# One-expert network: first layer two and second layer four steps behind the transpose, with an unread product of the identity ahead of each

## The reference

```python
scores = jnp.einsum('bsh,he->bse', x, wr) + br
expert_id = jnp.argmax(scores, axis=-1)
h = jnp.einsum('bsh,ehf->ebsf', x, w1) + b1[:, None, None, :]
h = jax.nn.gelu(h, approximate=False)
y = jnp.einsum('ebsf,efh->ebsh', h, w2) + b2[:, None, None, :]
one_hot = jax.nn.one_hot(expert_id, E, dtype=x.dtype)
out = jnp.einsum('ebsh,bse->bsh', y, one_hot)
...
x = x + _L1_ffn_ref(_layernorm(x, axis=-1), L1_ffn_wr, L1_ffn_br, L1_ffn_w1, L1_ffn_b1, L1_ffn_w2, L1_ffn_b2)
```

## Time and profile before

| | us |
|---|---|
| median of 3 runs (1870.96 to 1874.24) | 1872.3 |
| the profiled execution, its own time | 1877.03 |
| its span, first to last instruction | 1875.2 |
| share of the span in which PE, DVE, POOL, ACT are busy | 86%, 76%, 75%, 51% |

### The profile page before, as it was taken

How to read it: one execution, slowest core, us unless ns; L and a number is a source line. 1 busy time by engine, 2 the same in 40 slices (tenths; PEclk the granted TensorE clock), 3 DMA queues, 4 the chain that set the end, 5 groups by cost and what they waited for, 6 DMA issues and landing times. The chain is left out here.

```text
span 1875.2 us, 63422 instructions
## 1 busy us (share of the span) xinstructions
PE 1620.9 (86%) x24719; PEld 1365.9 (73%) x24719; DVE 1422.6 (76%) x3215; ACT 952.6 (51%) x2012; POOL 1408.6 (75%) x1270
## 2 busy tenths in 40 slices
PE   4999999999989364999999999999997688277776
PEld 3888888777778253778888888888886588277676
DVE  6988888888876914889898888888885756755554
ACT  3777887777763323454454544444443610344443
POOL 3887787988975554899999998888885267766654
PEclk9999999999999576999999999999999789588888
DMA  8000050000000414444444343433342364522211
GB/s 256 12 10 9 9 190 14 20 17 17 18 8 1 135 38 123 114 115 116 122 108 108 96 97 97 97 97 97 97 98 49 92 216 145 171 65 62 61 57 35
DMA packets 155077, 154.08 MB, mean 82 GB/s; under 512 B 37246, under 2 KB 106944, under 8 KB 154160
## 3 DMA queue, kind: packets, MB, share of 16 engines
q1 hardware_dynamic: 128912, 125.14, 24.7%
q0 software_dynamic: 6704, 15.61, 2.9%
q10 hardware_dynamic: 19312, 11.48, 2.3%
HBM read 58.77 MB, written 26.71 MB: 46 GB/s over the span
## 5 line engine op out<-in xcount | busy, mean ns | idle before, releaser
L1455 POOL TENSOR_TENSOR wa_rot<-wa_rot,wa_cross 128x1024 f32<-128x1024 f32 x128 | 306.9, 2397 | 44.1 <-DVE wa_cross L1673 43.0
L417 POOL TENSOR_TENSOR sa_sd<-sa_sd,sa_mx 128x1024 f32<-128x1024 f32 x128 | 245.2, 1916 | 78.2 <-DVE sa_mx L665 77.8
L1670 DVE TENSOR_TENSOR wa_rot<-wa_ps_qk,cos 128x1024 f32<-128x1024 f32 x128 | 155.6, 1216 | 36.8 <-PE wa_ps_qk L1521 36.7
L1620 ACT COPY wa_pt<-wa_ps_svt 128x1024 f32<-128x1024 f32 x64 | 64.9, 1015 | 220.7 <-PE wa_ps_svt L1557 220.7
L665 DVE TENSOR_REDUCE sa_mx<-sa_sd 128x16 f32<-128x1024 f32 x128 | 154.8, 1209 | 0.0
L1461 POOL TENSOR_TENSOR wa_sd<-wa_sd,wa_mx 128x1024 f32<-128x1024 f32 x64 | 121.8, 1904 | 34.2 <-DVE wa_mx L1686 33.8
L545 PEld LDWEIGHTS sa_ps_o<-sa_vbd,sa_pt 128*64 128x64 f32 x4096 | 135.0, 138 | 11.5 <-issue 8.1
L1521 PE MATMUL wa_ps_qk<-wa_xt,l_wk 128*128 128x128 f32 x1024 | 134.5, 286 | 9.7 <-DVE wa_cross L1673 9.5
L545 PE MATMUL sa_ps_o<-sa_vbd,sa_pt 128*64 128x18 f32 x4096 | 139.2, 210 | 1.8 <-DVE sa_o L694 1.8
L1521 PE MATMUL wa_ps_qk<-wa_xt,l_wq 128*128 128x128 f32 x1024 | 134.2, 285 | 6.4 <-DVE wa_cross L1673 4.1
L534 PE MATMUL sa_ps_st<-ident,sa_sd 128*128 128x128 f32 x1024 | 135.8, 276 | 3.7 <-ACT sa_sd L606 1.5
(11 more groups left out here) (313 smaller groups left out, 4307.0 us busy)
## 6 DMA issues: line engine op xcount, KB each, us to landing
wa_whole<-wa_rot SPq DMA_DIRECT2D x1024, 64.0 KB, 2.0
choice_dram<-sa_zero_rows SPq DMA_DIRECT2D x32, 256.0 KB, 3.2
choice<-choice_dram ACTq DMA_DIRECT2D x22, 256.0 KB, 4.0
x_res<-in_x_dram SPq DMA_DIRECT2D x16, 256.0 KB, 6.7
sa_ctx_t<-in_ctx_t_dram SPq DMA_DIRECT2D x64, 64.0 KB, 1.8
c_index<-in_index_dram SPq DMA_DIRECT2D x2, 2048.0 KB, 7.7
xn_dram<-c_xn SPq DMA_DIRECT2D x16, 256.0 KB, 3.0
cs_ctx_t<-in_ctx_t_dram SPq DMA_DIRECT2D x16, 256.0 KB, 2.9
```

The lines of the kernel that those rows point to most:

```text
L417: pool.tensor_tensor(sd[:, v % 4], sd[:, v % 4], mx[:, v % 4].unsqueeze(2).to_broadcast([P, H0, SEQ]), ALU.subtract).then_inc(sub_ready, 1)
L1455: pool.tensor_tensor(rot[n][:, v % 2], rot[n][:, v % 2], cross[n][:], ALU.add)\
L1670: dve.tensor_tensor(rot[n][:, v % 2].rearrange("p f j t -> p (f j) t"), src.rearrange("p f j t -> p (f j) t"), bc(k.cos[:], 1, 2 * QUADS), ...
```

## The change

The first layer moves from one to two steps behind the transpose, the second from two to four. The transposed tile, the hidden layer and `ps_h` get four buffers instead of two (`ps_x`, `ps_y` and the weights keep theirs), and the waits for free buffers move with them. In front of each layer, between the wait for a free buffer and the wait for the data, stands a product of the identity with itself, which goes to the place in PSUM that the layer then overwrites; nobody reads it. DVE's final add moves from three to four steps behind, to stay with the second layer.

```diff
-        xt = sb("xt", [P, 2, P])
-        hid = sb("hid", [P, 2, FF, P])
+        xt = sb("xt", [P, 4, P])
+        hid = sb("hid", [P, 4, FF, P])
-        ps_h = [c.enter_context(nc.psum_tensor(f"m1_h{n}", [P, FF, P], F32)) for n in range(2)]
+        ps_h = [c.enter_context(nc.psum_tensor(f"m1_h{n}", [P, FF, P], F32)) for n in range(4)]
...
+            def keep_on(room):
+                pe.matmul(room, k.ident[:], k.ident[:], start=True, stop=True)
...
             def hidden(t, v):
+                if late(t, 4):
+                    pe.wait_ge(hid_ready, t - 3)
+                keep_on(ps_h[v % 4][:, 0])
                 pe.wait_ge(xt_ready, t + 1)
                 pe.wait_ge(wt_ready, t + 1)
-                if late(t, 2):
-                    pe.wait_ge(hid_ready, t - 1)
                 for f in range(FF):
-                    mm = pe.matmul(ps_h[v % 2][:, f], w1[:, v % 4, f * P:(f + 1) * P], xt[:, v % 2], start=True, stop=True)
+                    mm = pe.matmul(ps_h[v % 4][:, f], w1[:, v % 4, f * P:(f + 1) * P], xt[:, v % 4], start=True, stop=True)
...
             def output(t, v):
-                pe.wait_ge(hid_ready, t + 1)
                 if late(t, 2):
                     pe.wait_ge(y_ready, t - 1)
+                keep_on(ps_y[v % 2][:, 0:P])
+                pe.wait_ge(hid_ready, t + 1)
                 for f in range(FF):
...
-                for stage, behind in ((transpose, 0), (hidden, 1), (output, 2)):
+                for stage, behind in ((transpose, 0), (hidden, 2), (output, 4)):
...
-            pipeline(pe, NS, step, 2, DEEP)
+            pipeline(pe, NS, step, 4, DEEP)
...
             def x_copy(t, v):
                 act.wait_ge(xt_made, t + 1)
-                if late(t, 2):
-                    act.wait_ge(h_made, t - 1)
+                if late(t, 4):
+                    act.wait_ge(h_made, t - 3)
...
             def gelu(t, v):
                 act.wait_ge(h_made, t + 1)
-                if late(t, 2):
-                    act.wait_ge(y_made, t - 1)
+                if late(t, 4):
+                    act.wait_ge(y_made, t - 3)
...
-                for stage, behind in ((x_copy, 0), (gelu, 1)):
+                for stage, behind in ((x_copy, 0), (gelu, 2)):
...
-            for i in range(NS + 3):
+            for i in range(NS + 4):
...
-                if i >= 3:
-                    add_up(i - 3)
+                if i >= 4:
+                    add_up(i - 4)
```

More of the change, by code:

```diff
@@ L2289, in hidden @@
             def hidden(t, v):
+                if late(t, 4):
+                    pe.wait_ge(hid_ready, t - 3)
+                keep_on(ps_h[v % 4][:, 0])
                 pe.wait_ge(xt_ready, t + 1)
                 pe.wait_ge(wt_ready, t + 1)
-                if late(t, 2):
-                    pe.wait_ge(hid_ready, t - 1)
                 for f in range(FF):
-                    mm = pe.matmul(ps_h[v % 2][:, f], w1[:, v % 4, f * P:(f + 1) * P], xt[:, v % 2], start=True, stop=True)
+                    mm = pe.matmul(ps_h[v % 4][:, f], w1[:, v % 4, f * P:(f + 1) * P], xt[:, v % 4], start=True, stop=True)
                 mm.then_inc(h_made, 1)
             def output(t, v):
-                pe.wait_ge(hid_ready, t + 1)
                 if late(t, 2):
                     pe.wait_ge(y_ready, t - 1)
+                keep_on(ps_y[v % 2][:, 0:P])
+                pe.wait_ge(hid_ready, t + 1)
                 for f in range(FF):
-                    mm = pe.matmul(ps_y[v % 2][:, 0:P], hid[:, v % 2, f], w2[:, v % 4, f], start=(f == 0), stop=(f == FF - 1))
+                    mm = pe.matmul(ps_y[v % 2][:, 0:P], hid[:, v % 4, f], w2[:, v % 4, f], start=(f == 0), stop=(f == FF - 1))
                 mm.then_inc(y_made, 1)
             def step(i, u):
-                for stage, behind in ((transpose, 0), (hidden, 1), (output, 2)):
+                for stage, behind in ((transpose, 0), (hidden, 2), (output, 4)):
                     if has(i - behind, NS):
                         stage(i - behind, (u - behind) % DEEP)
-            pipeline(pe, NS, step, 2, DEEP)
+            pipeline(pe, NS, step, 4, DEEP)
         @block.scalar
@@ L2316, in x_copy @@
                 act.wait_ge(xt_made, t + 1)
-                if late(t, 2):
-                    act.wait_ge(h_made, t - 1)
-                act.copy(xt[:, v % 2], ps_x[v % 2][:, 0:P]).then_inc(xt_ready, 1)
+                if late(t, 4):
+                    act.wait_ge(h_made, t - 3)
+                act.copy(xt[:, v % 4], ps_x[v % 2][:, 0:P]).then_inc(xt_ready, 1)
             def gelu(t, v):
                 act.wait_ge(h_made, t + 1)
-                if late(t, 2):
-                    act.wait_ge(y_made, t - 1)
+                if late(t, 4):
+                    act.wait_ge(y_made, t - 3)
                 for f in range(FF):
-                    op = act.activation(hid[:, v % 2, f], ps_h[v % 2][:, f], ACT.Gelu, bias=b1[:, v % 4, f:f + 1])
+                    op = act.activation(hid[:, v % 4, f], ps_h[v % 4][:, f], ACT.Gelu, bias=b1[:, v % 4, f:f + 1])
                 op.then_inc(hid_ready, 1)
             def step(i, u):
-                for stage, behind in ((x_copy, 0), (gelu, 1)):
+                for stage, behind in ((x_copy, 0), (gelu, 2)):
                     if has(i - behind, NS):
                         stage(i - behind, (u - behind) % DEEP)
-            pipeline(act, NS, step, 1, DEEP)
+            pipeline(act, NS, step, 2, DEEP)
         @block.vector
```

## The result

The changed kernel takes 1887.2 us (median of 4 runs, 1883.0 to 1889.6) where the kernel before takes 1872.4 (median of 4 runs, 1871.0 to 1874.2): a ratio of 1.0074, 95% interval 1.0058 to 1.0089, slower by some 14 us. The forecast was 1904: the sign is right, the size more than twice what was measured.

A forecast was written before the change was run, and what follows sets the result against it. It took late TensorE results beside gathers, above POOL's 2.58 us floor, to bound the step. Added passes cost 0.45 us a step, 32 us over 71 steps: 1877.0 + 32 = 1909, less 4.7, 1904; range 1842 to 1932.

The forecast's parts named there:

- What bounds the kernel: Stage's step: 3.14 us against POOL's floor of 2.58, because TensorE's results come late at full clock beside the gathers.
- The formula: TensorE's passes: 4.74 per us during POOL's 2.58 us, the rest at 8.9; 3.57 us a step after; chance 0.45.
- the term of 32 us: Identity products: 4 more passes a step at 0.112 us, 0.45 us a step, over 71 steps 32 us slower.
- the price at nothing: Identity products before the layers: lower bound, no cost if they fall into TensorE's waits of 17.5 + 37.5 us.
- DVE's part: DVE's loop: final add now behind the weight copy, 1.35 us after the result; counted as nothing in the sum.
- the four buffers' slack of 1.0 us: Weight copy before the first layer: 1.0 us of slack instead of 2.5; where results are later, next thing late.
- DVE's order: Rival, DVE's add behind the weight copy: 3.8 us a step with results 4.9 late, +47 us, 1919; chance 0.13.
- The distance: Transpose to first layer, and between layers: 3.3 us of lateness to spare against 0.5; gain 0 to 39 us.
- The slack wins: Rival, waits of gelu and add: slack covers most lateness, POOL paces; -39 us, 1833, with half 1853; chance 0.25.
- The clock: Rival, TensorE in the stage: products fill idle time, clock stays at 2.4 GHz, ends near POOL's floor; chance 0.07.
- The ends: Start and tail of the stage: two more iterations of lag, estimated under 3 us each.
- The signs that were named for being right: Stage's step near 3.6 us, gelus and adds microseconds late, TensorE near 5 to 6 passes per us, POOL idle before scatters.

## Why the prediction was wrong, and what it had right

**What bounds the kernel: right in the main.** Late results beside the gathers held the step at 3.14 us, above POOL's 2.58. That "results come late when TensorE runs at full clock beside the gathers" is too wide. In the same trace the m_h of 1702.39 to 1703.55, at a granted clock of 1.00 (1700 to 1703.6 us) and with gathers still to come, is used 0.04 us after its end:

```profile
1702.39 1.16 PE L2295 MATMUL m_h<-m_xt,m_wt 128*128 128x128 f32 x8 [0.76 <-ACT m_xt L2319]
...
1703.59 1.14 ACT L2326 ACTIVATE m_hid<-m_h,m_wt 128x128 f32<-128x128 f32 x4
```

Without indirect gathers the same program runs at (1777.03 - 1644.88) / 70 = 1.89 us a step, first to last scatter, which is its 17 passes at 0.112.

**The formula: wrong, and with it the term of 32 us.** The step that failed is the one that let "4.74 passes per us come through during POOL's 2.58 us" and the sentence that the products "go through the same queue as the results that others wait for". The throughput of a stretch in which TensorE itself waits for results is a consequence of the waits, not a limit: 8.4 per us passed beside the gathers when each product was issued three times. The formula gives 2.58 + (29 - 12.2) / 8.9 = 4.47 us a step with 29 passes; 3.38 was measured for the kernel with three of each product. That it met the present step within 0.02 was no test: its 4.74 and its 2.58 come from that same stretch. Products in front of the waits cost 2.6 us alone (0.14%) and 0.15 to 0.24% in the other pairs of kernels, 3 to 4.5 us instead of 32, as long as TensorE has waits to put them into (each of these differences is hardly larger than its own uncertainty): the price at nothing, the lower of the bounds named, was nearly right. Where it has none the price is 0.40 us a step, near the 0.45 of the working.

**DVE's part, counted at nothing: wrong.** The step is "I count nothing for it in the sum: it is the same lateness that the formula holds already". It isn't the same: the copy and the add now wait for the same late result one behind the other. The rows after show both ends of it, the add 1.27 us behind the copy and TensorE's new 26.7 us for m_wt. The text named the four buffers' slack of 1.0 us and what is late next; it priced it at zero. Freed of it alone the changed kernel falls from 1.0074 to 0.9995, 15 us.

**The rival "DVE's order"** had the place right and the price wrong: +47 us, since it took every second result to be 4.9 us late. POOL has 14 long waits in 70 steps, and they are 1.1 us longer on average than before.

**The distance** was bounded from 0 to -39 us and is worth -4.9 with everything else out of its way. "The slack wins" falls as a size, although its condition, that "most results are under 3.3 us late", was met. In the trace before, 61 of 71 gelus and 50 of 71 final adds start less than 3.3 us after the modelled end of their matmul, and still POOL keeps 17 waits above 1.5 us, with a mean of 2.59, in the kernel with the longer distance and eight weight buffers. In the kernel with eight buffers and products the m_y of the stall shown is known 1.66 us after POOL's gather has ended (1707.48 less 1705.82). Whether still more slack would spare such a pause no run shows.

**The clock**: the rival didn't come true. The Trainium skill, "TensorE: Matmul & The Clock Gate", section "Why this matters for your kernels", advises against idle gaps, since they cost clock. The trace agrees as to the clock: with three of each product the granted clock is 1.00, against 0.85 in the earlier trace rows. But the stage didn't end near POOL's floor: the changed kernel's clock rose to 0.90 with a step of 3.25 us, and with eight weight buffers it rose from 0.87 to 0.95 with no shorter step. That a higher clock alone brings nothing isn't shown, since every run that raised it added passes.

**The ends** cost 9.5 - 8.0 = 1.5 us, within the "under 3".

A path through the kernels puts the parts in order, each ratio to the kernel before; the steps are differences of ratios whose intervals are some 0.12 to 0.18% wide to each side:

| kernel | ratio | what the step adds, as argued | us |
|---|---|---|---|
| before | 1 | | |
| distances 2 and 4, weights always early | 0.9974 | the distance | -4.9 |
| four weight buffers, add first | 1.0004 | first layer waits for weights | +5.6 |
| add behind the copy | 1.0050 | POOL waits for the copy too | +8.6 |
| the products: the changed kernel | 1.0074 | | +4.5 |

The second step of the table also moves the add; that it is the first layer's wait is read from the rows, 1.5 against 50.8 us of idle time for m_wt, and no run took that wait out alone.

So the forecast of +32 was made of one term some seven to twelve times too large; a loss of 14 us and a gain of 5 were left out, and the errors partly cancel. That the sign came out right is luck: with the weights out of the way the distance and the products together give 0.9995, no loss at all. The signs that were named for being right came half: POOL idle before its scatters and 6.1 passes per us, but a step of 3.25 us and not 3.6.

## What to carry to other kernels

When a pipeline's distance grows, count the buffers of everything that crosses it: here xt and hid went from two to four, but the weights, which must live from the first layer to the second, kept their four, and an engine that works in order put the refill in front of the work that others waited for. A throughput read where an engine waits is not a rate; test it with work that nobody needs before pricing anything by it. Work put into waits is nearly free until the waits are full.

## What the runs showed of the hardware

Beside indirect gathers on POOL, TensorE's results are known late, in the stall of the earlier trace rows by 5.85 us after the matmul's modelled end. As many rows a step as plain loads of consecutive rows, from POOL through the same queue with the same 6704 packets and 15.61 MB, leave them prompt (0.03 us), and take 87 us off the kernel (0.9536 of 1878.1) with no other edit; part of that is POOL's own shorter step, 1.89 us instead of 2.58. The scatters by row list, still there, don't do it by themselves. The Trainium skill, "SBUF — State Buffer", section "Who interferes with whom", states that TensorE waits on nobody. That section is on SBUF's ports; read more widely, the loads' form could not matter to TensorE, and these two runs (0.9536 and 0.9526) speak against reading it so. What in the gather holds the results back, the row list, the scattered rows or POOL's longer instruction (0.97 us against 0.57), and whether it is the matmul or its signal that comes late, no run here tells; that stays open. It is also not settled what sets the number of long waits (14 to 22 in the kernels with indirect gathers, 32 with three of each product).
